# Moving where TensorE issues maxima products, values and projections in a fused attention and MoE kernel, with routing of eight tiles at a time

## The reference, cut to what matters

```python
x = x + tanh(g_xattn) * xattn(layernorm(x), ctx)        # 32 batches of 128 x 512, 8 heads of 16
x = x + tanh(g_ffn) * ffn(layernorm(x))                 # 4096 tokens of 512

# xattn, for each batch
q, k, v = Wq x1 + bq, Wk x2 + bk, Wv x2 + bv            # 8 heads, head size 16, 512 positions
out = softmax(q k^T / 4) v

# ffn
h = rmsnorm(x); probs = softmax(h @ router_w)           # 8 experts
keep the two largest of each token, normalised
out = sum over the two of silu(h Wg) * (h Wu) @ Wd  +  the same for one shared expert
```

## Time and profile before

| | |
|---|---|
| median of 3 runs | 1387.68 us (1385.4 to 1391.44) |
| profiled execution, its time | 1386.7 us |
| its span, first to last instruction | 1384.8 us |
| busy: PE, DVE, ACT, POOL | 1288.3, 975.1, 871.8, 861.5 us |
| reductions of maxima (DVE L1129) | 512, 615.0 us |
| exponentials (ACT L1413) | 1024, 552.4 us |

### The profile page before, as it was taken

One profiled execution on the slowest core, in us unless ns is written; L12 is line 12 of the kernel. 1 busy time (PEld: TensorE's weight loads), 2 busy tenths in 40 slices (PEclk: granted clock), 3 DMA queues, 4 the chain that ended last, 5 costly groups with the idle time before them and its releaser, 6 DMA issues.

```text
span 1384.8 us, 34397 instructions
## 1 busy us (share of the span) xinstructions
PE 1288.3 (93%) x12274; PEld 682.2 (49%) x12274; DVE 975.1 (70%) x1661; ACT 871.8 (63%) x1720; POOL 861.5 (62%) x1267
## 2 busy tenths in 40 slices
PE   2899999999999999999999989799999999999997
PEld 0233333333333333333333323587788888888886
DVE  5989889999999998989999877457654333333332
ACT  2488888888888888888888768333334333333332
POOL 8647777678787878877887643442114555555553
PEclk7799999999999999999999999999999999999999
DMA  7677887778888888788888773676555998885665
GB/s 187 185 197 227 224 241 220 207 227 214 201 223 207 213 218 227 191 222 210 218 217 221 162 185 90 161 161 149 127 175 105 214 216 193 178 189 110 108 110 81
DMA packets 167522, 256.65 MB, mean 185 GB/s; under 512 B 31717, under 2 KB 65132, under 8 KB 167358
## 3 DMA queue, kind: packets, MB, share of 16 engines
q1 hardware_dynamic: 149102, 217.08, 59.0%
q0 software_dynamic: 18256, 37.38, 14.9%
HBM read 141.06 MB, written 112.27 MB: 183 GB/s over the span
## 4 chain that ended last, share of the span: by engine, by line
PE 61%; DVE 12%; issue 10%; DMA 7%; POOL 3%; ACT 3%; SPq 2%; POOLq 1%; DVEq 0%; ACTq 0%
PE m_banks L956 21%; PE bank L913 12%; PE bank L882 10%; DVE row_max L1129 8%; PE m_banks L860 7%; PE bank L838 3%; PE bank L888 3%; DMA arena<-parts_q 2%; PE bank L844 2%; ACT arena L1413 2%; DMA arena<-ht_d 1%; POOL xs L780 1%; PE bank L978 1%; SPq L458 1%; PE bank L869 1%
## 5 line engine op out<-in xcount | busy, mean ns | idle before, releaser
L1129 DVE TENSOR_REDUCE row_max<-m_banks 128x2 f32<-128x1024 f32 x512 | 615.0, 1222 | 76.1 <-PE m_banks L860 67.9
L1413 ACT ACTIVATE arena<-bank 128x512 f32<-128x512 f32 x1024 | 552.4, 606 | 73.4 <-PE bank L882 71.9
L882 PE MATMUL bank<-arena 112*32 112x512 bf16 x4096 | 336.2, 382 | 6.6 <-ACT arena L1413 3.2
L913 PE MATMUL bank<-arena 128*32 128x512 f32 x2048 | 280.2, 598 | 0.4 <-ACT arena L1421 0.3
L882 PEld LDWEIGHTS bank<-arena 112*32 112x32 bf16 x4096 | 114.7, 95 | 266.0 <-ACT arena L1413 132.4
L792 POOL DMA_INDIRECT out<-xs,ids x71 | 112.3, 1582 | 173.4 <-ACT xs L1495 135.7
L860 PE MATMUL m_banks<-arena 48*128 48x512 bf16 x1024 | 177.4, 393 | 39.6 <-DVE row_max L1129 25.7
L956 PE MATMUL m_banks<-w_ring,h_hi 128*128 x568 | 183.0, 403 | 0.0
L1484 ACT ACTIVATE arena<-m_banks 128x256 f32<-128x256 f32 x103 | 39.5, 384 | 186.9 <-PE m_banks L956 186.9
L860 PEld LDWEIGHTS m_banks<-arena 48*128 48x128 bf16 x1024 | 40.4, 93 | 175.2 <-DVE row_max L1129 79.9
L1337 DVE TENSOR_TENSOR arena<-arena,m_banks 128x256 f32<-128x256 f32 x71 | 29.9, 421 | 116.5 <-ACT arena L1484 116.5
(11 more groups left out here) (182 smaller groups left out, 1999.9 us busy)
## 6 DMA issues: line engine op xcount, KB each, us to landing
arena<-parts_k SPq DMA_DIRECT2D x128, 192.0 KB
arena<-parts_q SPq DMA_DIRECT2D x128, 192.0 KB
parts_k<-arena SPq DMA_DIRECT2D x64, 256.0 KB, 6.6
parts_q<-arena SPq DMA_DIRECT2D x64, 256.0 KB, 5.1
pv_d<-arena SPq DMA_DIRECT2D x32, 512.0 KB, 4.3
split_d<-staged SPq DMA_DIRECT2D x30, 512.0 KB, 9.1
w_ring<-split_d SPq DMA_DIRECT2D x60, 256.0 KB, 3.9
arena<-in_w SPq DMA_DIRECT2D x36, 256.0 KB, 8.4
```

Of the source, the lines that this page charges most:

```text
L882: last = nc.tensor.matmul(out[c, :], k_stack[b % 3][0:SHIFTED, h, kt * P + c.start:kt * P + c.stop], q_stack[b % 3][0:SHIFTED, h, :], star ...
L913: last = nc.tensor.matmul(pv_ps[2 * DH * j:2 * DH * (j + 1), :], v_ones[b % 3][:, kt, GROUP * g + j, :], probs[pair % 3][:, j, :], start=( ...
L1129: nc.vector.reduce_max(pair, m_ps[(STEPS * b + u) // 2 % M_PAIRS], AX_X).then_inc(s_mx, 1)
L1413: nc.scalar.activation(probs[group % 3][:, j, :], bank_of["scores", b, s], ACT.Exp, scale=float(DH) ** -0.5).then_inc(s_exp, 1)
```

## The change

- On TensorE, a group of four steps was E, E, M, M, then tokens, logits or a projection if the group has one, then E, E, X if it has one, V. It is now E, E, M, V, E, E, M, then tokens, logits or a projection, then X. The slots on ScalarE at which projections, turned tokens and values are taken are not changed.
- The high row of the maxima is made by ScalarE (`maxima_high`, after the exponentials of steps 4 and 20) and VectorE makes only the second (`maxima_row`).
- On VectorE the small operations of the moments and of the routing have steps of their own; routing works on 8 tiles at a time in place of 4, so that the attention part has 3 of 4 rounds in place of 7 of 8 (with one round of places after it before). The last round covers 8 tiles, and the scatters of 16 tiles, in place of 8, come after the attention part.

```diff
-MOMENTS2_AT = 10
-MOMENTS_AT = 27
-RECIP_AT = 16
+MOMENTS2_AT = (9, 11, 11, 11, 11)
+MOMENTS_AT = (27, 31, 31, 31, 31)
+RECIP_AT = 19
-CHUNK = 4
+CHUNK = 8
-QUIET_AT = 20
+ROUTE_FROM = 23
+ROUTE_AT = (3, 3, 7, 13, 15, 15, 19, 23, 25, 29, 29)
...
                 for b in range(B - 2 * CHUNK):
-                    if i == min(b + 10, B - 1):
+                    if i == b + CHUNK + 6:
                         scatter(b)
...
                     if is_b(i + 1):
                         max_scores(i + 1, s)
+                    if s == 0 and is_b(i - 1):
+                        values(i - 1, STEPS // GROUP - 1)
+                    if s and is_b(i):
+                        values(i, s // GROUP - 1)
+                    if is_b(i):
+                        exp_scores(i, s + 2)
+                        exp_scores(i, s + 3)
+                    if is_b(i + 1):
                         max_scores(i + 1, s + 2)
                     if s == TURN_TOKENS_AT and is_b(i - 3):
                         turn_tokens(i - 3)
...
                     if s in PROJECT_AT and is_b(i + PROJECT_AT[s][0]):
                         project(i + PROJECT_AT[s][0], PROJECT_AT[s][1])
-                    if is_b(i):
-                        exp_scores(i, s + 2)
-                        exp_scores(i, s + 3)
                     if s + 3 == MAX_AT[1] and is_b(i):
                         turn_maxima(i, 1)
                     if s + 3 == MAX_AT[0] and is_b(i + 1):
                         turn_maxima(i + 1, 0)
-                    if s == 0 and is_b(i - 1):
-                        values(i - 1, STEPS // GROUP - 1)
-                    if s and is_b(i):
-                        values(i, s // GROUP - 1)
...
-            def maxima_rows(b, half):
...
+            def maxima_row(b, half):
+                dve.wait_ge(s_mh, 2 * b + half + 1)
+                nc.vector.scalar_tensor_tensor(m_rows[half][:, 1, :], bank_of["maxima", b, half][0:GROUP * KT, 0:P], -1.0,
+                                               m_rows[half][:, 0, :], ALU.mult, ALU.subtract).then_inc(s_mr, 1)
...
-                    if s == MAX_AT[1] + 1 and is_b(i):
-                        run(maxima_rows(i, 1))
-                    if s == MAX_AT[0] + 1 and is_b(i + 1):
-                        run(maxima_rows(i + 1, 0))
                     if s % 2 == 0 and is_b(i + 1):
                         maximum(i + 1, s)
+                    if s == MAX_AT[1] + 2 and is_b(i):
+                        maxima_row(i, 1)
+                    if s == MAX_AT[0] + 2 and is_b(i + 1):
+                        maxima_row(i + 1, 0)
...
-                    if QUIET_AT <= s < QUIET_AT + 7:
-                        routed = [steps for steps in routed if next(steps, steps) is not steps]
...
+                    if s == ROUTE_FROM and i > CHUNK and (i - 2) % CHUNK == 0:
+                        routed = choices((i - 2) // CHUNK - 1)
+                    if s == ROUTE_FROM and i > CHUNK and (i - 4) % CHUNK == 0:
+                        routed = places((i - 4) // CHUNK - 1)
+                    advance(routed, ROUTE_AT.count(s))
...
-                if j == 0:
-                    run(places(N_CHUNKS - 2))
...
+            def maxima_high(b, half):
+                act_e.wait_ge(s_mt, 2 * b + half + 1)
+                if b:
+                    act_e.wait_ge(s_row[half], 2 * DMA * b)
+                nc.scalar.mul(m_rows[half][:, 0, :], bank_of["maxima", b, half][0:GROUP * KT, 0:P], -1.0).then_inc(s_mh, 1)
...
+                    if s == MAX_AT[1] + 1 and is_b(i):
+                        maxima_high(i, 1)
+                    if s == MAX_AT[0] + 1 and is_b(i + 1):
+                        maxima_high(i + 1, 0)
                     if s in HIGH_AT and is_b(i + 3):
                         high_part(i + 3, HIGH_AT.index(s))
```

More of the change, by code:

```diff
@@ L287, in build @@
         s_mt = sem("s_mt")
+        s_mh = sem("s_mh")
         s_mr = sem("s_mr")
@@ L1012, in _ @@
                         turn_maxima(i + 1, 0)
-                    if s == 0 and is_b(i - 1):
-                        values(i - 1, STEPS // GROUP - 1)
-                    if s and is_b(i):
-                        values(i, s // GROUP - 1)
-                    if s + 3 == COUNT_SLOT and i >= 7 and (i - 7) % CHUNK == 0:
-                        count_choices((i - 7) // CHUNK)
+                    if s + 3 == COUNT_SLOT and i > CHUNK and (i - 3) % CHUNK == 0:
+                        count_choices((i - 3) // CHUNK - 1)
                     if i == B - 1 and s == FIRST_JOB_AT:
@@ L1056, in chain @@
                     if n:
+                        yield
                         dve.wait_ge(s_dve, done)
-                        yield
                     ins = op()
@@ L1070, in advance @@
                 for _ in range(n):
-                    next(steps)
+                    next(steps, None)
             def first_value(r, b):
@@ L1253, in _ @@
                     if s == RECIP_AT and is_b(i - 1):
                         invert(i - 1)
[L1255 to L1258, removed]
+                    if s == MOMENTS_AT[0] and is_b(i + 5):
+                        first_moments = moments(i + 5)
+                    if s in MOMENTS_AT:
+                        advance(first_moments, MOMENTS_AT.count(s))
@@ L1259, in _ @@
+                    if s == MOMENTS2_AT[0] and is_b(i - 2):
+                        second_moments = moments2(i - 2)
+                    if s in MOMENTS2_AT:
+                        advance(second_moments, MOMENTS2_AT.count(s))
                     if s == LOGITS_AT + 1 and is_b(i - 3):
                         take_logits(i - 3)
[L1261 to L1264, removed]
@@ L1269, in _ @@
+                    advance(routed, ROUTE_AT.count(s))
+                    if s == COUNT_SLOT and i > CHUNK and (i - 3) % CHUNK == 0:
+                        take_counts((i - 3) // CHUNK - 1)
                     if i == B - 1 and s in SHARED_PARTS_AT:
@@ L1451, in _ @@
                         exponential(i, s)
+                    if s == MAX_AT[1] + 1 and is_b(i):
+                        maxima_high(i, 1)
+                    if s == MAX_AT[0] + 1 and is_b(i + 1):
+                        maxima_high(i + 1, 0)
                     if s in HIGH_AT and is_b(i + 3):
                         high_part(i + 3, HIGH_AT.index(s))
-                    if s == EXP_SLOT and i >= 7 and (i - 7) % CHUNK == 0:
-                        exponentials((i - 7) // CHUNK)
+                    if s == EXP_SLOT and i > CHUNK and (i - 3) % CHUNK == 0:
+                        exponentials((i - 3) // CHUNK - 1)
                     if s == STAGE_AT and 0 <= i + 2 < len(STAGED):
```

15 lines of the change are left out of this document (1 added, 14 removed).

## The result

The changed kernel takes 1653.28 us, median of four runs (1651.79 to 1655.48), against 1386.54 us beside it: a ratio of 1.1917, 95% interval 1.1883 to 1.1951. The forecast was 1614 with a range of 1560 to 1670.

What follows compares the result with a forecast made beforehand. TensorE, busy 93%, bounds the kernel; the new order makes it wait for ScalarE. Turns of 33.5 us against 25.96 add 197 us in 26 turns, plus 19, 9 and tail 2: 227 on 1386.7, about 1614 us, range 1560 to 1670.

Steps and rivals of the forecast that it cites:

- P to the next score tile: TensorE, from a projection's start until the next score tile can start: 2.36 us, where the projection alone takes 0.88.
- E4 to V: From the score tile of step 4 to the values product, behind ScalarE's values copy: 1.77 us, a wait of 0.9.
- the high row: ScalarE's new maxima row ahead of the values copy: about 0.2 us, bounds 0.1 and 0.35.
- A turn of 33.5 us: Full attention turn: 24.6 + 3.5 + 1.6 + 1.5 + 1.8 + 0.5 us, against 25.96 before.
- The signs named beforehand: ScalarE idle 1.5 to 2.5 us before evacuations, score tiles waiting 1.2 to 1.5, reciprocals every 33 to 34.
- a rival with a chance of 0.04: Lower clock from TensorE's waits: a fifth of the attention at 1.2 GHz adds 150 us, 1765 in all; chance 0.04.
- the last sign of a wrong forecast: Forecast wrong if the attention's granted clock falls below full.
- that row covered: VectorE's second maxima row waits for ScalarE's row, which is ready while VectorE still reduces: no cost.
- The tail: After the attention, the table is gathered 10.2 us later; its turning in job 24 costs 2 us, between 0 and 10.
- the second visit to the M shape: TensorE enters the shape of the maxima products twice a group, where before it did so once: 0.2 us more.
- the late units and the early values: Late projections and tokens stall TensorE 3.5, 1.6 and 1.5 us a turn; earlier values products wait for their copy, 1.8.
- the halved routing: VectorE has at least 7.5 us a turn to spare, so halved routing gains nothing further; whole routing costs some 0.9.

Runs made afterwards that it cites:

- tensor_only: The kernel before with the changed order on TensorE alone (E, E, M, V, E, E, M, unit, X), nothing else changed: 1626.53 us, ratio 1.1774.
- slots_moved: The changed kernel with TensorE untouched and ScalarE's slots for projections and turned tokens moved two steps later: 1511.92 us, ratio 1.0954.
- only_units_late: The kernel before with tokens, logits and projections behind the second two score tiles (E, E, M, M, E, E, unit, X, V): 1453.36 us, ratio 1.0500.
- only_apart: The kernel before with each group's second M behind the second two score tiles (E, E, M, unit, E, E, M, X, V): 1401.35 us, ratio 1.0114.
- square of orders: Four TensorE orders with M apart: units early, V last 1401 us; units early, V early 1455; units late, V last 1473; units late, V early 1627.
- routing_only: The changed kernel with TensorE's old order and both maxima rows on VectorE at their old place: 1387.94 us, ratio 1.0012.
- mended: routing_only with scatters of tiles 16 to 23 in turns 30 and 31, reciprocals at step 16, table turned in job 26: 1409.18 us, ratio 1.0077.
- values_back: The changed kernel with units and values at their old place on TensorE, only the M apart (E, E, M, unit, E, E, M, X, V): 1546.23 us, ratio 1.1193.

## Why the prediction was right

**The mechanism and its main terms were right.** By its steps: P to the next score tile 2.36 us, measured 2.36; the next tile after that 0.49, measured 0.49 (590.31 to 590.80); E4 to V 1.77, measured 1.80. Within that, the high row takes 0.25 us but holds the copy behind it for only 0.16 (599.62 to 599.78), where the sum had 0.2. V then waits 0.73 us in the mean (46.1 us, 63 times), where the sum had 0.9. A turn of 33.5 us was forecast and 33.77 is the steady turn. That the order of TensorE carries it is shown by tensor_only (242 of 267 us); that it is ScalarE's slots and not the place of the units is shown by slots_moved, which gave 141 us back with TensorE untouched. The signs named beforehand came out: waits of 2.2, 2.4 and 1.9 us before L1392, L1396 and L1430, of 1.2 us before the score tiles, and a steady turn between 33 and 34 us.

**The time is 39 us above the forecast.** Turns 3 to 29 took 34.58 us each (169.61 to 1068.68), not 33.5: 28 us. Some 7 us of it are the steady turn. The other 21 are longer turns, for which the forecast had no term. The view of all turns splits them in two:

- Six turns of 35.3 to 37.5 us have a mean granted clock of 0.91 or 0.95. They hold 14.8 of the 21 us, and their matmuls are busy for 10.3 us more than in as many steady turns. I had held the clock for a rival with a chance of 0.04, at a fifth of the attention; it came, but small: 0.98 over 150 to 1000 us, where only_units_late has 1.00. By its letter the last sign of a wrong forecast, a clock of the attention below full, was thus seen (0.99 over turns 3 to 29, before 1.00), although the mechanism stands. One of the low stretches follows the wait for the read of q. That the lower level followed a wait there agrees with the Trainium skill, page TensorE: Matmul & The Clock Gate, section HAM oscillation, in kind.
- Eight turns at the full clock hold the other 6.3 us, the longest of them 35.1 to 35.3 us. All eight lie in rounds of routing, with up to 42 operations on VectorE, and in the three longest TensorE waits 1.2 to 1.5 us for the second row of the maxima. The forecast had called that row covered and put nothing on routing. Three of the six turns above lie in such rounds as well, so the split between clock and routing is not clean.

The late read of q, which is plain in the chain of the turn of 36.90 us, is 1.5 us of TensorE's waits in turns 3 to 29.

**The tail** was put at 2 us between 0 and 10, and is 8.4 (165.06 less 156.63). The number is inside, the mechanism is not. The forecast looked for it in the table that comes later, and TensorE did not wait for the table at all. In its place ScalarE's waits for the loads of the shared jobs' tokens grew by 7.2 us, from 16.4 to 23.6. Why those loads come later is not shown. The remaining 5 us lie outside these turns and the tail, in the first and last turns.

**Mode changes.** The sum gave the second visit to the M shape 0.2 us and took 0.16 off for V. The net of 0.3 us a turn is 0.65 in only_apart, little beside the 7.6 of the change. The Trainium skill, page TensorEngine Tiling (Array Packing), section Key Properties, says that a change of tiling mode drains TensorE, which is the kind of step that this is. No run here tells how much of the 0.65 us is that drain.

**What the forecast got right for an incomplete reason.** It priced the late units and the early values as separate terms, 6.6 and 1.8 us a turn. The square of orders shows that the first term exists at that size only because V is early: the late units cost 172 us with V early (1627 less 1455) and 72 with V last. The sum was right since both moves were in the change; the expectation for only_units_late, which took the term over alone, was off by a factor of two.

**VectorE.** The forecast gave the halved routing no gain, as its cover was large. In the old order it is worth little too. The 0.2 us of a turn without routing in routing_only is the place of the reciprocal, as mended shows. Over turns 3 to 29 the mean is 25.68 us against 25.96, 0.3 us a turn with the reciprocal in it, and it was gone again by the first routed tile.

## What to carry to other kernels

Where two engines run programs written out in order, read the change of one against the other's program: for each unit that moves, look for where its consumer waits for it and what stands finished behind that wait. Price a stall with the instruction that follows in the new order, since one piece of independent work (here 0.86 us of V) decides between a wait of 0.4 and one of 1.3 us, and two moves that each take a cover away can cost more than their sum. Check whether spreading work evenly takes a wait away before paying for it: in only_apart the second change of shape cost 1%, and VectorE's waits for maxima products did not shrink (77.2 us after, 67.9 before).

## What the runs showed of the hardware that was not expected

- The granted clock fell to its lower level in seven short stretches of turns 3 to 29 of the changed kernel, in none of these turns of the kernel before. One stretch stands right behind the wait for the read of q; in the other five turns with a low stretch TensorE's waits are 1.4 us at most, no longer than in the steady turns, which have four such waits, TensorE busy for 80% in the profile and a clock of 1.00. So the length of the waits alone does not tell where the clock falls. The mean over 150 to 1000 us was 0.98 in the changed kernel, 0.95 in values_back and 1.00 in only_units_late.
- In routing_only ScalarE stood 7.7 and 7.0 us, and VectorE 5.8 us beside the first, before work whose inputs from TensorE were there and for which the profile names no releaser. The first of ScalarE's two waits lay beside sixteen scatters one after another on GpSimd. Moving eight tiles' scatters into the attention removed the waits and the kernel was no faster. That the scatters cause them was not isolated.
